# A top-1 expert stage on one Trainium2 core: every expert on all 576 tokens, or each on its 90 slots

## The chip, the cores and the metric

The kernel runs on one core of a Trainium2 chip (trn2). The metric is the device time of one execution in microseconds (us). Engine names are those of the profile: PE does matrix products, PEld loads PE's stationary operand, DVE is the vector engine, ACT the scalar engine, POOL the GpSimd engine, SP issues most DMAs. PSUM is the memory that PE writes, in 8 banks of 512 float32 columns; everything else lies in SBUF.

## The reference

The model is a small vision tower: 16 images of 36 patches give 576 tokens of 64 values, and four blocks of attention and feed-forward work follow, each with a layer norm behind it. The change is in the first feed-forward stage (`_L0_ffn_ref`), a top-1 mixture of 8 experts with a capacity:

```
C = max(1, math.ceil(CAPACITY_FACTOR * T / E))        # 1.25 * 576 / 8 = 90
idx = jnp.argmax(probs, axis=-1)
pos = (jnp.cumsum(one_hot, axis=0) * one_hot).sum(-1).astype(jnp.int32) - 1
kept = pos < C
buf = jnp.zeros((E, C, D), dtype=h.dtype).at[idx, pos_safe].set(x, mode='drop')
hmid = jax.nn.relu(jnp.einsum('ecd,edf->ecf', buf, w1) + b1[:, None, :])   # D 64, F 256
ybuf = jnp.einsum('ecf,efd->ecd', hmid, w2) + b2[:, None, :]
y_tok = ybuf[idx, pos_g] * (prb * kept)[:, None]
y = jnp.nan_to_num(y, nan=0.0, posinf=10000.0, neginf=-10000.0)
```

## The kernel before

The kernel is one program, `tower`, with the instructions of each engine written out by hand in the order in which the engine runs them. Semaphores (`S["..."]`) order the engines among themselves; nothing is scheduled for it. Activations lie transposed, 64 features by 288 tokens twice: the first 288 tokens on partitions 0 to 63 and the others on 64 to 127 (`rows(h)`). In token order there are 6 tiles of 96 tokens (`TT` is 96).

Each norm goes the same way: ACT squares the sum in PSUM (L905), PE sums the squares (L424), ACT takes a root (L910), DVE a reciprocal (L1118), PE spreads it over the partitions (L432, in `spread`), DVE multiplies (L1123). `idle(n, bank)` (L417) is n matmuls of 512 columns on zeros whose result nobody reads.

The first expert stage is `ffn(0, HP)`. The router gives logits (L450), DVE finds each token's expert (`top_first`) and its softmax gate, and PE counts with a triangular matrix how many tokens chose the same expert before (L493, L496); a token beyond 90 gets gate 0. The gates are split in three bf16 parts, turned by PE (L504) and copied by DVE (L1150). Then all 8 experts work on all 576 tokens, in 16 chunks of 128 hidden values: `up` (L464) multiplies, ACT applies relu (L925), `gate` (L471) spreads the expert's gate over 128 partitions in PSUM, DVE multiplies (L1203), `down` (L477) adds into one PSUM bank. DVE replaces values that aren't finite (L1315 to L1322, the guard), and PE adds the centred result to the residual (L655). The next norm begins there.

POOL computes tables for a recurrence that comes two stages later (`lru_*`: L357 to L377, 45 instructions, one after the other by semaphore; L357 works on 576 columns, most others on 1 to 36). Ahead of them in its order stand the rope tables (L350, L352) and `gates32(0)` (L325), which waits until DVE has copied the turned gates of this stage.

## Time and profile before

| | |
|---|---|
| median of 3 runs | 156.04 us (155.33 to 158.31) |
| span of the profiled execution | 153.6 us |
| PE busy | 139.1 us, 91% |
| DVE, ACT, POOL busy | 97.4, 71.6, 34.8 us |

The time of a run also holds what lies before and behind the span; against the median that is 2.4 us. Times in the trace count from the start of the span. A PE matmul on float32 is two records. An instruction's record holds a fixed part in which the next one has already begun, so rates are read from the starts of a series or from its whole length, not from the mean of one.

### The profile page before, as it was taken

To read this page: it belongs to the slowest core of one execution; us is meant where nothing else is said; L and a number is where in the kernel's file an instruction comes from. 1 tells how busy PE (TensorE), PEld (TensorE's weight loads), DVE (VectorE), ACT (ScalarE), POOL (GpSimd) and SP (SyncE) were. 2 spreads that over 40 slices of the span, in tenths; PEclk is the share of its full clock that TensorE was granted. 3 is DMA by queue.
4 is the path that set the end of the run, shared out by engine and by line. 5 is a ranking of instruction groups with operands and counts; after the bars stand their busy time and mean duration, and the time that the engine had idled before them with its cause. 6 is when DMAs were issued, how large, how long until landed. Compare 5 with 4: busy or idle time off the path is not lost.

```text
span 153.6 us, 2957 instructions
## 1 busy us (share of the span) xinstructions
PE 139.1 (91%) x1132; PEld 72.8 (47%) x1145; DVE 97.4 (63%) x299; ACT 71.6 (47%) x136; POOL 34.8 (23%) x91
## 2 busy tenths in 40 slices
PE   6999999899999999698999977999899999999970
PEld 1455465645454344164355333547354464654550
DVE  6405858755466736756677899755758468314992
ACT  3645951675647010059244202434881366458452
POOL 8704000037777100002600004300087000000000
PEclk9999999999999999999999999999999999999999
DMA  5999991000000000000002000000000000000001
GB/s 154 353 426 382 264 358 54 0 0 2 6 0 2 0 0 0 4 0 0 0 3 59 0 2 0 0 4 0 4 0 0 0 0 6 0 0 4 0 0 38
DMA packets 3716, 8.17 MB, mean 53 GB/s; under 512 B 1579, under 2 KB 1707, under 8 KB 3574
## 3 DMA queue, kind: packets, MB, share of 16 engines
q1 hardware_dynamic: 3390, 7.87, 15.0%
q8 instruction: 9, 0.15, 0.4%
q10 hardware_dynamic: 312, 0.11, 0.3%
q14 instruction: 5, 0.04, 0.1%
HBM read 7.61 MB, written 0.15 MB: 51 GB/s over the span
## 4 chain that ended last, share of the span: by engine, by line
PE 65%; DVE 22%; ACT 5%; issue 4%; DMA 2%; DVEq 0%; ACTq 0%
PE ps L477 10%; PE ps L464 9%; PE ps L417 9%; PE ps L471 4%; PE ps L424 3%; DVE scores L1383 3%; DVE residual L1504 3%; PE ps L432 2%; DMA weights_sb<-weights 2%; DVE patch_sb L1496 2%; PE ps L582 2%; PE ps L574 2%; PE ps L446 2%; DVE scores_rest L1404 2%; ACT hidden L925 1%
## 5 line engine op out<-in xcount | busy, mean ns | idle before, releaser
L417 PE MATMUL ps<-idle_operand 128*128 128x512 bf16 x111 | 31.7, 394 | 4.7 <-DVE scores L1383 1.6
L1203 DVE TENSOR_TENSOR hidden_gated<-hidden,ps 128x576 f32<-128x576 f32 x28 | 19.7, 750 | 10.5 <-PE ps L471 10.5
L925 ACT ACTIVATE hidden<-ps,weights_sb 128x576 f32<-128x576 f32 x28 | 19.6, 738 | 9.9 <-PE ps L464 8.2
L917 ACT ACT_TABLE_LOAD x16 | 20.5, 1283 | 0.3
L417 PEld LDWEIGHTS ps<-idle_operand 128*128 128x128 bf16 x124 | 10.4, 102 | 17.3 <-issue 3.7
L905 ACT ACTIVATE squares<-ps 128x288 f32<-128x288 f32 x7 | 2.9, 411 | 28.9 <-PE ps L672 8.4
L477 PE MATMUL ps<-hidden_gated,weights_sb 128*64 128x288 f32 x112 | 16.3, 418 | 0.0
L325 POOL CAST combine_parts_T<-combine_parts_T 64x288 f32<-64x288 bf16 x3 | 1.3, 418 | 55.3 <-DVE combine_parts_T L1150 55.3
L464 PE MATMUL ps<-h,weights_sb 64*128 64x288 f32 x80 | 13.0, 436 | 0.7 <-ACT hidden L925 0.4
L1115 DVE COPY centred<-ps 128x288 f32<-128x288 f32 x7 | 3.2, 457 | 11.9 <-ACT squares L905 11.9
L477 PEld LDWEIGHTS ps<-hidden_gated,weights_sb 128*64 128x64 f32 x112 | 6.7, 135 | 7.0 <-DVE hidden_gated L1203 2.7
L856 PE MATMUL ps<-weights_sb,hidden 128*128 128x256 f32 (+2 forms) x28 | 9.8, 473 | 0.0
L464 PEld LDWEIGHTS ps<-h,weights_sb 64*128 64x128 f32 x80 | 6.7, 185 | 5.9 <-ACT hidden L925 3.2
L1383 DVE TENSOR_REDUCE scores<-ps 128x32 f32<-128x512 f32 (+1 forms) x13 | 7.7, 652 | 0.7 <-PE ps L724 0.7
L471 PE MATMUL ps<-combine_parts_T,selectors 128*128 128x288 bf16 x40 | 7.4, 289 | 0.0
L424 PEld LDWEIGHTS ps<-consts_sb,squares 128*96 128x96 f32 x48 | 4.7, 164 | 3.9 <-ACT squares L905 3.4
L432 PE MATMUL ps<-consts_sb,rstd 96*64 96x96 f32 x108 | 6.2, 253 | 0.1
L464 PE MATMUL ps<-xn,weights_sb 64*128 64x288 f32 x32 | 5.5, 446 | 0.5 <-ACT hidden L925 0.4
L432 PEld LDWEIGHTS ps<-consts_sb,rstd 96*64 96x64 f32 x108 | 4.7, 136 | 2.4 <-DVE rstd L1118 2.1
L856 PEld LDWEIGHTS ps<-weights_sb,hidden 128*128 128x128 f32 (+1 forms) x28 | 4.6, 183 | 2.4 <-issue 1.6
L389 POOL TENSOR_TENSOR patch_sb<-scores,top 128x288 f32<-128x288 f32 (+1 forms) x2 | 1.6, 782 | 18.2 <-DVE top L1392 18.1
L471 PEld LDWEIGHTS ps<-combine_parts_T,selectors 128*128 128x128 bf16 x40 | 3.0, 97 | 5.3 <-issue 1.9
(309 smaller groups left out, 235.7 us busy)
## 6 DMA issues: line engine op xcount, KB each, us to landing
patch_sb<-patches SPq DMA_DIRECT2D x6, 288.0 KB, 5.5
weights_sb<-weights SPq DMA_DIRECT2D x1, 1108.0 KB, 10.1
weights_sb<-weights SPq DMA_DIRECT2D x1, 717.0 KB, 15.1
weights_sb<-weights SPq DMA_DIRECT2D x1, 689.0 KB, 13.8
weights_sb<-weights SPq DMA_DIRECT2D x1, 640.0 KB, 7.6
weights_sb<-weights SPq DMA_DIRECT2D x1, 512.0 KB, 13.5
...
```

The source lines that it names most:

```text
L417: mm(PS[:, bank, :], idle_in[:, 0:P], idle_in[:, :], start=True, stop=True)
L424: last = mm(psVar[:, 2 * t:2 * t + 2], SQ[:, cols(t)], c("mean"), start=True, stop=True)
L432: last = mm(dst[rows(h), cols(t)], RS[:, at + 2 * t + h:at + 2 * t + h + 1].to_broadcast([TT, D]), c("ident", TT)[:, 0:TT], start=True, st ...
L464: last = mm(PS[:, z + h, 0:HALF], w1[rows(h), ch, :], src[rows(h), :], start=True, stop=True)
L471: last = mm(PS[:, bank + h, 0:HALF], sel[:, g, h, :], CT3[:, :], start=True, stop=True)
L477: last = mm(PS[rows(h), YB, 0:HALF], w2[:, ch, :], HG[:, ch % GRING, h, :], start=False, stop=(ch == chunks - 1), skip_group_check=True)
L856: return mm(y3(q, a, b), tok3(q, ch), wd[:, ch, a * E:b * E], start=False, stop=(ch == 1), skip_group_check=True)
L917: act.activation(warm[:, tables[0]:tables[0] + 1], warm[:, 0:1], func)
L925: act.activation(HR[:, at % RING, :, :], two(ZA if ch % 2 == 0 else ZB), func, bias=w(f"b1_{n}")[:, ch:ch + 1]).then_inc(S["act_out"], 1)
L1203: dve.tensor_tensor(HG[:, at % GRING, :, :], HR[:, at % RING, :, :], two(GATE_AT[n][ch]), ALU.mult)\
L1383: dve.tensor_reduce(SC[:, j, :, 8 * g:8 * g + keys].rearrange("p h s -> p s h"), PS[:, n % 4, 0:keys * D].rearrange("p (s h d) -> p s h d" ...
L1504: ins = dve.tensor_reduce(R[0:p, q, a:b], YM[0:p, q, a:b, :], AX, ALU.add)
```

## The change

Each expert now works on its 90 slots alone. Experts 0 to 3 lie on partitions 0 to 63 and experts 4 to 7 on 64 to 127.

- Slot numbers: the counting matmuls get one more (L645 of the new kernel) that adds 1024 times the expert's number, so that the count read at a token's own expert is a number that names expert and slot. DVE takes it out (two instructions).
- Gather: for each of the 6 token tiles a one-hot matrix of 96 tokens by 720 slots is made by comparing a table `IO` with the slot numbers (5 on DVE, 1 on POOL); PE multiplies the normalised tokens by it (`dispatch`). The tokens in token order come from 3 new PE transposes and 6 ACT copies that also scale them.
- Experts: `up` and `down` on 90 columns per expert; the biases come in through matmuls of 4 rows and of 1 row (`before_up`, `before_down`). ACT takes one half of the relu, DVE the other.
- Return: PE spreads the slot numbers over the partitions (`slot_b`), ACT copies them, and 8 one-hot matrices of 90 slots by 576 tokens are made (`put_rows`, 5 on DVE, 3 on POOL); `bring_back` multiplies by them. DVE first bounds the experts' outputs to finite values (`finite`), and the gate is multiplied behind it.
- The splitting and turning of this stage's gates goes, and with it `gates32(0)`. Two DMAs of small bias rows and one of `IO` (270 KB) are added, and `w1_0` is loaded once instead of on both halves (512 KB less).

```diff
-    ("gate_w", 2 * E), ("gb0", E), ("b1_0", 2 * E), ("b2_0", P), ("w1_0", 2 * E * P),
+    ("gate_w", 2 * E), ("gb0", E), ("w1_0", E * P),
...
+DT = HR[0:CAP, :, :, :]
...
+DS = [x_flat[0:TT, i * SLOTS:(i + 1) * SLOTS] for i in range(IN_X)] \
...
+XK = sb("x0_tok", [TT, 2 * NT, D])
...
+SLB = KP[:, :].rearrange("p (h n) -> p h n", h=2)
+XD = sb("x0_slots", [P, SLOTS // 2])
+HD = [[x[:, 0:4 * CAP] for x in pair] for pair in ((U, B1), (B2, UC))]
...
+PUT_DVE, PUT_POOL = [0, 1, 4, 3, 6], [5, 2, 7]
+POOL_TILE = 2 * NT - 1
...
+def put_rows(engine, e):
+    return engine.tensor_scalar(DT[:, e, :, :].rearrange("p h n -> p (h n)"), token_ids(),
+                                c("slot_id", CAP)[:, e:e + 1], None, ALU.is_equal)
...
+    sp.dma_start(IO[:, :], iota).then_inc(S["iota0"], 16)
...
-    gates32(0)
...
+    pool.wait_ge(S["iota0"], 16)
+    pool.wait_ge(S["slot"], 1)
+    pool.tensor_scalar(DS[POOL_TILE], IO[:, :], slot[:, POOL_TILE:POOL_TILE + 1], None, ALU.is_equal)\
+        .then_inc(S["disp_pool"], 1)
+    pool.wait_ge(S["slot_in"], 1)
+    for e in PUT_POOL:
+        put_rows(pool, e).then_inc(S["put_pool"], 1)
     gates32(1)
...
-        bank = MB if k == 4 else ZA
+        bank = {1: YB, 4: MB}.get(k, ZA)
...
-            gate(0, G)
...
-            for pair in range(1, E - 2):
-                gate(pair, G, 2 * pair - 1)
-                down(2 * pair - 2)
-                down(2 * pair - 1)
...
-            gate(E - 2, ZA)
...
-            gate(E - 1, ZB)
-            for ch in range(chunks - 6, chunks):
-                down(ch)
...
+    def experts0():
...
+        def before_up(s):
+            for g in range(2):
+                mm(PS[:, 2 * s + g, 0:4 * CAP].rearrange("p (j n) -> p j n", j=4),
+                   BR0[0:4, (2 * s + g) * P:(2 * s + g + 1) * P],
+                   c("ident")[0:4, 0:4].unsqueeze(2).to_broadcast([4, 4, CAP]),
...
+        def dispatch(i):
+            if i == POOL_TILE:
+                pe.wait_ge(S["disp_pool"], 1)
+            else:
+                pe.wait_ge(S["disp_dve"], i + 1)
+            for g in range(2):
+                last = mm(psD[rows(g), :], XK[:, i, :], DS[i][:, g * slots:(g + 1) * slots],
...
+        def up(s):
+            pe.wait_ge(S["xd_in"], s + 1)
+            for r in range(2):
+                for ch in range(2):
+                    for g in range(2):
+                        j = 2 * r + ch
+                        last = mm(PS[:, 2 * s + g, j * CAP:(j + 1) * CAP], w1[rows(g), 2 * s + r, ch, :],
+                                  XD[rows(g), (2 * s + r) * CAP:(2 * s + r + 1) * CAP],
...
+            last.then_inc(S["z0"], 1)
+        def before_down(s):
+            mm(psS[s].rearrange("p (g f) -> p g f", g=2), ones[32:33, 0:CAP], staged(BR0[32:33, :])[:, s],
...
+        def down(s):
+            for g in range(2):
+                pe.wait_ge(S["h0_act" if g == 0 else "h0_dve"], s + 1)
+                for r in range(2):
+                    e = 4 * g + 2 * s + r
+                    for ch in range(2):
+                        last = mm(psS[s][:, (2 * g + r) * D:(2 * g + r + 1) * D], HD[s][g][:, (2 * r + ch) * CAP:(2 * r + ch + 1) * CAP], w2[:, e, ch, :],
...
+            last.then_inc(S["ys_done"], 1)
+        def bring_back(s):
+            pe.wait_ge(S["ys_in"], s + 1)
+            for g in range(2):
+                for r in range(2):
+                    e = 4 * g + 2 * s + r
+                    sem, count = putter(e)
+                    pe.wait_ge(S[sem], count)
+                    for h in range(2):
+                        last = mm(psBack[rows(h), :], YS[:, e, :], DT[:, e, h, :],
...
+        idle(4, YB)
...
+        pe.wait_ge(S["onehot"], 1)
...
+        mm(psN, tri[0:1, 0, :], cb("slot_base", 1).rearrange("p (i e) -> p i e", e=E),
...
+        mm(psN, tri[:, 1, :], ohb[:, :, :], start=False, stop=False, skip_group_check=True)
+        for k in range(2 * NT - 1):
+            later = 2 * NT - 1 - k
+            last = mm(psN[:, k + 1:2 * NT, :], tri[:, 0, :],
+                      ohb[:, k, :].unsqueeze(1).to_broadcast([TT, later, E]),
...
+        last.then_inc(S["counted"], 1)
+        pe.wait_ge(S["rows0"], 32)
+        pe.wait_ge(S["x0_ready"], 2 * NT)
+        before_up(0)
+        pe.wait_ge(S["slot"], 1)
+        for h in range(2):
+            for t in range(NT):
+                i = h * NT + t
+                last = mm(PS[:, ZB + h, cols(t)], slot[:, i:i + 1].to_broadcast([TT, P]), c("ident", TT)[:, 0:TT],
...
+        last.then_inc(S["slot_b"], 1)
+        for i in range(3):
+            dispatch(i)
+        before_down(0)
+        dispatch(3)
+        dispatch(4)
+        pe.wait_ge(S["slot_in"], 1)
+        before_up(1)
+        dispatch(5).then_inc(S["xd_done"], 1)
+        up(0)
+        up(1)
+        pe.wait_ge(S["gate0"], 1)
+        for t in range(NT):
+            for h in range(2):
+                last = mm(psBC[rows(h), cols(t)], m6[3][0:TT, 2 * t + h:2 * t + h + 1].to_broadcast([TT, D]),
...
+        last.then_inc(S["gate0_b"], 1)
+        pe.wait_ge(S["w_f0b"], 16)
+        down(0)
+        pe.wait_ge(S["gate0_in"], 1)
+        before_down(1)
+        down(1)
+        bring_back(0)
+        bring_back(1).then_inc(S["back"], 1)
...
+        last = pe.transpose(PS[0:TT, ZA, t * P:(t + 1) * P], XC[:, cols(t)], c("ident"))
+    last.then_inc(S["x0_t"], 1)
     spread(1)
-    pe.wait_ge(S["w_f0b"], 16)
-    pe.wait_ge(S["hp"], 2)
-    ffn(0, HP)
+    experts0()
+    residual("ident")
     idle(2, ZA)
...
+    act.wait_ge(S["x0_t"], 1)
+    act.wait_ge(S["rs"], 2)
+    for t in range(NT):
+        for h in range(2):
+            act.activation(XK[:, h * NT + t, :], PS[0:TT, ZA, t * P + h * D:t * P + (h + 1) * D], ACT.Copy,
+                           scale=RS[:, 2 * t + h:2 * t + h + 1]).then_inc(S["x0_ready"], 1)
     table(ACT.Exp)
     act.wait_ge(S["exp_in"], 1)
     act.activation(ex[0:TT, :, :], t8[0][0:TT, :, :], ACT.Exp).then_inc(S["exp_out"], 1)
-    act.wait_ge(S["w_f0"], 16)
-    hidden(0, ACT.Relu, range(2 * E))
+    act.wait_ge(S["slot_b"], 1)
+    act.activation(SLB[:, :, :], two(ZB), ACT.Copy).then_inc(S["slot_in"], 1)
     table(ACT.Sqrt)
+    act.wait_ge(S["xd_done"], 1)
+    for s in range(2):
+        act.activation(XD[:, 2 * s * CAP:2 * (s + 1) * CAP], psD[:, 2 * s * CAP:2 * (s + 1) * CAP], ACT.Copy)\
+           .then_inc(S["xd_in"], 1)
+    for s in range(2):
+        act.wait_ge(S["z0"], s + 1)
+        act.activation(HD[s][0], PS[:, 2 * s, 0:4 * CAP], ACT.Relu)\
+           .then_inc(S["h0_act"], 1)
+    act.wait_ge(S["gate0_b"], 1)
+    act.activation(PB[:, :], psBC, ACT.Copy).then_inc(S["gate0_in"], 1)
...
+    def experts0():
...
+        dve.wait_ge(S["counted"], 1)
+        link(dve.tensor_tensor(count, psN, ohb[:, :, :], ALU.mult))
+        dve.tensor_reduce(slot[:, :], count, AX, ALU.add).then_inc(S["slot"], 1)
+        dve.wait_ge(S["slot"], 1)
+        dve.wait_ge(S["iota0"], 16)
+        for i in range(POOL_TILE):
+            dve.tensor_scalar(DS[i], IO[:, :], slot[:, i:i + 1], None, ALU.is_equal).then_inc(S["disp_dve"], 1)
+        dve.wait_ge(S["exp_out"], 1)
+        link(dve.tensor_reduce(m6[2][0:TT, :], ex[0:TT, :, :], AX, ALU.add))
+        dve.reciprocal(m6[3][0:TT, :], m6[2][0:TT, :]).then_inc(S["gate0"], 1)
+        dve.wait_ge(S["slot_in"], 1)
+        def put(n):
+            put_rows(dve, PUT_DVE[n]).then_inc(S["put_dve"], 1)
+        def relu(s):
+            dve.wait_ge(S["z0"], s + 1)
+            dve.tensor_scalar(HD[s][1], PS[:, 2 * s + 1, 0:4 * CAP], 0.0, None,
+                              ALU.max).then_inc(S["h0_dve"], 1)
+        def finite(s):
+            dve.wait_ge(S["ys_done"], s + 1)
+            step(dve.tensor_scalar(YP[:, s, :], psS[s], 0.0, SAT, ALU.max, ALU.min))
...
+            sync()
+            dve.tensor_tensor(staged(YS[:, :, :].rearrange("p e d -> p (e d)"))[:, s], YP[:, s, :].rearrange("p (g f) -> p g f", g=2),
...
+                              ALU.add).then_inc(S["ys_in"], 1)
+        put(0)
+        put(1)
+        put(2)
+        relu(0)
+        put(3)
+        relu(1)
+        put(4)
+        finite(0)
+        finite(1)
+        dve.wait_ge(S["gate0_in"], 1)
+        dve.wait_ge(S["back"], 1)
+        step(dve.tensor_tensor(RY[:, :], psBack, PB[:, :], ALU.mult))
+        step(dve.tensor_scalar(nf[:, :], psBack, LIMIT_A, LIMIT_B, ALU.mult, ALU.mult))
+        sync()
+        link(dve.tensor_scalar(RX[:, :], nf[:, :], 1.0e4, None, ALU.mult))
+        dve.copy_predicated(RY[:, :], nf[:, :], RX[:, :]).then_inc(S["guarded"], 1)
...
     link(dve.tensor_reduce(m6[0][0:TT, :], lg[0:TT, :, :], AX, ALU.max))
+    top_first(None, lg, m6[0], t8[1], m6[1], TT, 2 * NT)
+    dve.tensor_tensor(in_order(ohb[:, :, :]), by_tile(t8[1][0:TT, :, :]), by_tile(col(m6[1], TT, 2 * NT)), ALU.is_equal)\
+       .then_inc(S["onehot"], 1)
     dve.tensor_tensor(t8[0][0:TT, :, :], lg[0:TT, :, :], col(m6[0], TT, 2 * NT), ALU.subtract)\
        .then_inc(S["exp_in"], 1)
     normalise(1, HP[:, :], "hp")
-    top_first(t8[2], lg, m6[0], t8[1], m6[1], TT, 2 * NT)
-    dve.tensor_copy(in_order(ohb[:, :, :]), by_tile(t8[2][0:TT, :, :])).then_inc(S["onehot"], 1)
-    dve.wait_ge(S["exp_out"], 1)
-    link(dve.tensor_reduce(m6[2][0:TT, :], ex[0:TT, :, :], AX, ALU.add))
-    link(dve.reciprocal(m6[3][0:TT, :], m6[2][0:TT, :]))
-    link(dve.tensor_tensor(comb[0:TT, :, :], t8[2][0:TT, :, :], col(m6[3], TT, 2 * NT), ALU.mult))
-    dve.wait_ge(S["counted"], 1)
...
-    link(dve.tensor_tensor(comb[0:TT, :, :], comb[0:TT, :, :], t8[1][0:TT, :, :], ALU.mult))
...
-    gate_hidden(0)
-    dve.wait_ge(S["y_done"], 2 * E)
-    dve.tensor_copy(RY[:, :], psY).then_inc(S["guard_read"], 1)
-    dve.wait_ge(S["guard_read"], 1)
-    step(dve.tensor_scalar(np_[:, :], RY[:, :], FMAX, 1.0e4, ALU.is_gt, ALU.mult))
-    step(dve.tensor_scalar(nm[:, :], RY[:, :], -FMAX, 1.0e4, ALU.is_lt, ALU.mult))
-    step(dve.tensor_scalar(nf[:, :], RY[:, :], 0.0, 0.0, ALU.mult, ALU.not_equal))
-    sync()
-    link(dve.tensor_tensor(np_[:, :], np_[:, :], nm[:, :], ALU.subtract))
-    dve.copy_predicated(RY[:, :], nf[:, :], np_[:, :]).then_inc(S["guarded"], 1)
...
```

On PE, in the middle of the stage, this stood in a row before (`up`, `gate`, `down` in turn):

```order
L464 MATMUL ps<-h,weights_sb 128x288 x4
L471 MATMUL ps<-combine_parts_T,selectors 128x288 x2
L477 MATMUL ps<-hidden_gated,weights_sb 64x288 x4
L464 MATMUL ps<-h,weights_sb 128x288 x4
L471 MATMUL ps<-combine_parts_T,selectors 128x288 x2
L477 MATMUL ps<-hidden_gated,weights_sb 64x288 x4
```

and this stands there now, from the counting to the first matmuls of `up`:

```order
L589 MATMUL ps<-consts_sb,bias_rows 128x360 x2
L661 MATMUL ps<-consts_sb,slot_of_token 128x96 x6
L600 MATMUL ps<-patch_sb,x_tok 64x360 x6
L616 MATMUL ps<-bias_rows,ones 90x256
L600 MATMUL ps<-patch_sb,x_tok 64x360 x2
L600 MATMUL ps<-hidden_gated,x_tok 64x360 x2
L589 MATMUL ps<-consts_sb,bias_rows 128x360 x2
L600 MATMUL ps<-hidden_gated,x_tok 64x360 x2
L610 MATMUL ps<-x_slots,weights_sb 128x90 x16
```

The last `dispatch` (on the tile that POOL makes) stands right ahead of `up`.

On POOL, behind the rope tables, this stood before:

```order
L350 TENSOR_SCALAR rope_tables<-consts_sb,weights_sb 128x36 x4
L352 TENSOR_TENSOR rope_tables<-rope_tables 128x36
L325 CAST combine_parts_T<-combine_parts_T 64x288
L357 TENSOR_SCALAR decay<-decay,lru_par 128x576
L358 COPY lru_sin_sb<-lru_par 128x1
```

and now:

```order
L391 TENSOR_SCALAR rope_tables<-consts_sb,weights_sb 128x36 x4
L393 TENSOR_TENSOR rope_tables<-rope_tables 128x36
L396 TENSOR_SCALAR decay<-decay,lru_par 128x576
L397 COPY lru_sin_sb<-lru_par 128x1
L398 TENSOR_SCALAR lru_t<-lru_par 128x1
```

Nothing now stands between the rope tables and the recurrence tables. Behind those, on POOL, the new work stands in a row:

```order
L415 TENSOR_SCALAR rot_out_c<-lru_cos,consts_sb 128x36
L416 TENSOR_SCALAR rot_out_s<-lru_sin_sb 128x36
L420 TENSOR_SCALAR hidden_gated<-slot_iota,slot_of_token 96x720
L303 TENSOR_SCALAR hidden<-kp,consts_sb 90x576 x3
L366 CAST combine_parts_T<-combine_parts_T 64x288
```

So POOL's part of the gather and of the return comes only when all recurrence tables are done.

## Rows read from the trace of the kernel before

**Rows 1.** The page: busy time by engine, and the granted clock in 40 slices.
```profile
PE 139.1 (91%) x1132; PEld 72.8 (47%) x1145; DVE 97.4 (63%) x299; ACT 71.6 (47%) x136; POOL 34.8 (23%) x91
...
PEclk9999999999999999999999999999999999999999
```
**Rows 2.** Groups by form, 26 to 56 us: count | busy us, mean ns | idle before.
```profile
L1203 DVE TENSOR_TENSOR hidden_gated<-hidden,ps 128x576 f32<-128x576 f32 x16 | 11.3, 750 | 7.3 <-PE ps L471 7.2
...
L464 PE MATMUL ps<-h,weights_sb 64*128 64x288 f32 x64 | 10.3, 435 | 0.3 <-DVE h L1123 0.2
L477 PE MATMUL ps<-hidden_gated,weights_sb 128*64 128x288 f32 x64 | 9.4, 419 | 0.0
```
**Rows 3.** Timeline of PE, 24 to 60 us: start, length, what.
```profile
27.73 0.71 PE L432 MATMUL ps<-consts_sb,rstd 96*64 96x96 f32 x12
...
30.38 0.22 PE L493 MATMUL ps<-onehot_bf,bconsts_sb 96*96 96x48 bf16 x1
...
42.91 1.24 PE L464 MATMUL ps<-h,weights_sb 64*128 64x288 f32 x8
44.08 0.42 PE L471 MATMUL ps<-combine_parts_T,selectors 128*128 128x288 bf16 x2
44.43 1.19 PE L477 MATMUL ps<-hidden_gated,weights_sb 128*64 128x288 f32 x8
45.55 1.24 PE L464 MATMUL ps<-h,weights_sb 64*128 64x288 f32 x8
...
54.61 0.75 PE L655 MATMUL ps<-guard_y,consts_sb 128*128 128x288 f32 x2 [0.17 <-DVE guard_y L1322]
```
**Rows 4.** Timeline of DVE, 24 to 60 us.
```profile
29.92 0.18 DVE L1303 CAST onehot_bf<-gate_tmp 96x48 bf16<-96x48 f32 x1
...
30.92 0.20 DVE L1309 TENSOR_SCALAR gate_tmp<-ps 96x48 f32<-96x48 f32 x1 [0.24 <-PE ps L496]
...
52.31 0.46 DVE L1315 COPY guard_y<-ps 128x288 f32<-128x288 f32 x1 [0.81 <-PE ps L477]
52.80 0.31 DVE L1317 TENSOR_SCALAR plus_inf<-guard_y 128x288 f32<-128x288 f32 x1
...
54.07 0.48 DVE L1322 COPY_PREDICATED guard_y<-nonfinite,plus_inf 128x288 f32<-128x288 int32 x1
```
**Rows 5.** Timelines of PE elsewhere, for rates: one series each.
```profile
7.54 3.12 PE L582 MATMUL ps<-patch_sb,weights_sb 128*64 128x288 f32 x23
...
22.36 1.98 PE L629 MATMUL ps<-kernel_T,v_sb 36*128 36x36 f32 x32 [0.36 <-DVE kernel_T L1258]
...
98.39 1.31 PE L757 MATMUL ps<-consts_sb,probs 128*128 128x128 f32 x10
...
126.77 2.11 PE L417 MATMUL ps<-idle_operand 128*128 128x512 bf16 x9 [0.16 <-issue]
```
**Rows 6.** Timeline of ACT: 4 copies that scale by a column.
```profile
149.06 1.12 ACT L1071 ACTIVATE out_sb<-residual,gate_col 64x64 f32<-64x64 f32 x4
```
**Rows 7.** Timeline of POOL: rope tables, and first and last of the recurrence.
```profile
12.92 0.26 POOL L352 TENSOR_TENSOR rope_tables<-rope_tables 128x36 f32<-128x36 f32 x1
...
33.46 1.72 POOL L357 TENSOR_SCALAR decay<-decay,lru_par 128x576 f32<-128x576 f32 x1
...
50.31 0.30 POOL L377 TENSOR_SCALAR rot_out_s<-lru_sin_sb 128x36 f32<-128x36 f32 x1
```
**Rows 8.** Timelines of DVE and PE, 13 to 18 us.
```profile
13.70 0.43 DVE L1225 TENSOR_SCALAR xn<-q_rot,weights_sb 128x288 f32<-128x288 f32 x1
14.28 1.24 PE L593 MATMUL ps<-xn,weights_sb 64*128 64x288 f32 x8
...
16.00 0.76 DVE L1246 TENSOR_TENSOR kp<-base_sb,rope_tables 128x576 f32<-128x576 f32 x1 [0.86 <-ACT base_sb L945]
17.46 0.76 DVE L1249 TENSOR_TENSOR k_rot<-kp,ks 128x576 f32<-128x576 f32 x1
```
**Rows 9.** Timelines of DVE and POOL, 94 to 98 us.
```profile
94.66 0.32 DVE L1396 TENSOR_TENSOR patch_sb<-top 128x160 f32<-128x160 f32 x1
94.70 0.87 POOL L389 TENSOR_TENSOR patch_sb<-scores,top 128x320 f32<-128x320 f32 x1
...
96.81 0.72 POOL L396 TENSOR_TENSOR patch_sb<-patch_sb,row_stat 128x320 f32<-128x320 f32 x1
```

More of the change, by code:

```diff
@@ L84 @@
 zero3 rows_c wo_c cen_c wr_gam wr_bet_mm wr_bet rows_zero still topped replaced filled idrep
+iota0 rows0 x0_t x0_ready slot slot_b slot_in disp_dve disp_pool xd_done xd_in z0 h0_dve h0_act ys_done ys_in
+put_dve put_pool gate0 gate0_b gate0_in back
 acc sq xc var sd rs bc hp xn
@@ L1195, in gate_hidden @@
             def gate_hidden(n):
-                chunks, gate_of = FFN[n]
-                for ch in range(chunks):
+                for ch in range(FFN[n]):
                     at = BASE[n] + ch
@@ L1666, in _pack, with _rows0 @@
     return pk
+def _rows0(b1, b2):
+    by_bank = b1.reshape(2, 2, 2, 2, P).transpose(2, 3, 1, 0, 4)
+    return np.concatenate([by_bank.reshape(4, 4 * P), b2.reshape(1, E * D)], 0).astype(np.float32)
 def kernel(**inputs):
@@ L1683 @@
         "maskk": mask,
+        "iota": np.tile((SLOT_STEP * np.arange(E)[:, None] + np.arange(CAP)[None, :] + 1).reshape(1, -1), (TT, 1))
+        .astype(np.float32),
+        "rows0": _rows0(i["L0_ffn_b1"], i["L0_ffn_b2"]),
         "bias3": np.tile(i["L3_ffn_bd"].T.reshape(1, -1), (3, 1)).astype(np.float32),
```

139 lines of the change are left out of this document (75 added, 64 removed).

## The prediction

> **What bounds the kernel now.** I read the page first. PE is busy for 91% of the span, DVE for 63%, and the granted clock is at its full level (2.4 GHz) in every slice [rows 1]. A busy share doesn't say what ends last, so the chain of waits came next: in this stage it runs through `up`, `gate` and `down` (L464, L471, L477) almost without a break. The groups by form say why: `up` and `down` are 64 records each, with 0.3 us and nothing of idle time ahead of them, while DVE sits idle for 7.3 us before L1203 [rows 2]. So the stage is PE's. The timeline gives its frame: the first count starts at 30.38, the matmul that ends the stage (L655) at 54.61, and between them one turn of the loop takes 45.55 - 42.91 = 2.64 us [rows 3]. Behind the last `down` come 2.3 us of guard, from 52.31 to 54.61 [rows 3, 4]. The result's place is the start of the centre matmul; what lies behind it is the same work in both kernels, on the same chain, and I move it as a block.
>
> **Rates.** L582 runs pairs of 288 float32 columns on half-width tiles: 12 matmuls (one record of 24 is missing) in 3.12 us, less a tail of 0.2 (L493 lasts 0.22 for almost no columns), give 0.49 a pair, 1.7 ns a column [rows 3, 5]. Where columns are few, loading the stationary operand sets the pace: L757 has 128 columns on either side and takes (1.31 - 0.2) / 10 = 0.11 a record; L629 moves only 36 columns under 128-wide weights on alternating halves of the rows, and takes (1.98 - 0.2) / 32 = 0.056 [rows 5]. An idle matmul is (2.11 - 0.2) / 9 = 0.21 [rows 5]. The loop's turn holds 4 pairs (1.96) and two bf16 matmuls (0.24); the 0.44 left over fall on three changes of tile shape, 0.15 each [rows 3].
>
> A rule speaks against the change here: the Trainium skill, page TensorEngine Tiling (Array Packing), section Tiling Modes, says that changing the tiling mode drains the engine. The trace agrees in kind (0.15 us over at each change); the page gives no figure. With no cost for a change the sum below would be 1.8 us shorter.
>
> **Part 1, up to the slot numbers.** Three transposes stand ahead of the spreading of the reciprocals, 3 x 0.11: it starts at 27.73 + 0.33 = 28.06 instead of 27.73 [rows 3] and lasts 0.5. Now 6 idle matmuls follow where 2 did: 1.27, so PE is ready to count at 29.85. The one-hot was ready at 30.10 [rows 4]; now a copy is folded into the comparison, and the subtraction for the exponential and the multiplication of L1123 stand behind it, about 0.2 + 0.2 + 0.4, so that it is there at about 29.3. The idle matmuls, not DVE, now hold up the count. From the first count to DVE's reading it were 30.92 - 30.38 = 0.54 [rows 3, 4]; with one more, 0.6. Two small DVE instructions make the slots: about 30.95. PE has 1.2 us of `before_up(0)` to do meanwhile. That one also needs ACT's six copies: four of that kind took 1.12, so 0.28 each [rows 6], from 28.6 at the latest to 30.3, when PE comes to them: just hidden. Were they later, each tenth would count.
>
> **Part 2, PE from there.** Each bias matmul of 360 columns is 0.61, although it has only 4 rows; each `dispatch` is a pair of 360 columns, 0.61.
> - `before_up(0)`: 0.15 + 1.22, from 30.25 to 31.6.
> - slot numbers, 12 records of 128-wide weights: 0.15 + 1.3, to 33.1.
> - six `dispatch` 3.67, `before_down(0)` 0.43, `before_up(1)` 1.22, five changes of shape 0.75: to 39.2.
> - hop to ACT and back (tail 0.2, a copy of 180 columns some 0.3, start 0.05): to 39.75. Nothing covers it.
> - `up`, 32 records at 0.056: to 41.5. Gates 0.15 + 0.5: to 42.15. The relus (some 0.5 on each engine) lie under these.
> - `down`, 32 records of 90-wide weights, 0.11 x 90 / 128 = 0.08: 2.5, with 0.43 of bias and three changes: to 45.55.
> - `bring_back`, 8 pairs of 288 columns: 0.15 + 3.92, to 49.6, and the tail to 49.8.
> - Guard: the copy out of PSUM goes; two readings of PSUM (0.46, the second about 0.39 behind the first), one 0.31, one 0.48, with the hops 1.7 [rows 4]: the centre matmul starts at 51.55.
>
> That is 54.61 - 51.55 = 3.05 us earlier. By the rates, the stage before was 32 pairs, 16 bf16 matmuls and one bias matmul, 18.1 us of columns; now it is 2.4 + 1.3 + 3.7 + 0.9 + 1.8 + 0.5 + 2.5 + 3.9 = 17.0. Gathering, returning and the biases eat what 720 rows of expert work instead of 4608 save.
>
> **Part 3, DVE and POOL in the stage.** Five comparisons of 720 columns: L1225, with two column operands on 288 columns, took 0.43 [rows 8], and L1317, with none, 0.31 [rows 4]. The bound for one is so 0.5 (double rate) to 0.9 (single), and even at 0.9 the five are ready at 31.9, 32.8, 33.7, 34.6 and 35.5, before PE wants each (33.3, 33.9, 34.5, 35.7, 36.3), each by at least 0.8. The matrices for the return and `finite` also fall before PE needs them: `finite(0)` starts at 43.8 and takes 1.3, PE wants it at 45.55. Where DVE falls back by a microsecond this shows at once.
> POOL makes one dispatch tile: 1.72 x 720 / 576 = 2.15 us [rows 7]. Its recurrence tables took 50.61 - 33.46 = 17.15 us [rows 7]. They don't wait for `gates32(0)` any more, so they start at 13.2, end at 30.35 undisturbed, and the tile is there at 33.1, where PE wants it at 38.6: 5.5 us of cover.
> The DMAs: 0.5 MB less, 0.27 more, and all queue behind what the beginning needs. Nothing.
>
> **Part 4, what the earlier start of POOL collides with.** At 13.2 the 1.72 us instruction of POOL (L357) now runs while DVE does L1225 at 13.70, for which PE's L593 at 14.28 waits directly [rows 8]. Before, DVE's work beside L357 was the multiplication out of PSUM. Can the two disturb each other? One place shows it: DVE's L1396, with two operands in SBUF, starts at 94.66, POOL's L389 at 94.70 and it takes 0.87, where the same size takes 0.72 at 96.81 [rows 9]. POOL gave way by 0.15. That DVE gives way when POOL is first no row shows. So the bounds for L1225: 0, and waiting for POOL's end (14.9 instead of 13.70), 1.2, of which PE feels 1.1. I take the upper one, since the one collision on record looks like waiting, not like sharing. `kp`, `ks` and `k_rot` (16.00 to 18.2) would meet short POOL instructions: 0.3 together. Sum 1.4 us lost at 14 to 18 us, against 3.05 won.
>
> The Trainium skill, page SBUF — State Buffer, section SBUF: two separate sides, states that GpSimd and DVE share a port pair under an exclusive lock, held for the whole instruction, against DVE instructions in a two-port mode or with two SBUF inputs; the loser blocks fully. The 0.15 us agree with it, and no row here shows its other direction. By this rule the upper bound holds; without it the lower.
>
> **Forecast.** 3.05 - 1.4 = 1.65 us off the span of 153.6; off the median of 156.04 (which holds 2.4 us around the span, untouched) that is 154.4 us.
>
> **Rivals.**
> - No collision: DVE's L1225 isn't held. Then 156.04 - 3.05 = 153.0. For it: no row of a delayed DVE instruction. Against it: rows 9.
> - Changes of shape are cheap when the next operands are ready: 0.05 instead of 0.15 at 12 of them, 1.2 less: 153.2 with the collision, 151.8 without. For it: `gate` waits on semaphores in the loop, which may be part of the 0.44.
> - POOL is late, slower than before. Every DVE instruction with two SBUF operands or at double rate between 13 and 36 us (some 9.5 us of them, 5 x 0.76 in 16 to 20 alone) holds POOL's chain for its length. Tables to 39.9, tile to 42.0, where PE wants it at 38.6 + 1.4 = 40.0: 2.0 more, 156.4. It decides from a tile at 41.7 on. Against it: POOL lost only 0.15 to a DVE instruction of 0.32, and gaps lie between DVE's.
> - Loads not hidden in `up` and `down`: columns come on top, 1.2 and 1.7 us: 157.3 with the collision, 155.9 without. Against it: L629's 0.056, which is under load plus columns.
> - That the change doesn't shorten the expert work can't be: `up` goes from 64 to 32 records and from 288 to 90 columns.
>
> **Chances.** Forecast 0.38, no collision 0.26, cheap changes 0.18, POOL late 0.10, loads exposed 0.08. A measurement of this kernel tells about 2%, 3.1 us, from no change: below 152.9 lie half of the second, two thirds of the third and a little of the first, 0.32 together; above 159.2 lies little, 0.03. The range from 151.5 to 156.9 leaves out about a tenth on either side.
>
> **What would show it.** The first matmul on `xn` (L593 before) starting at 15.4 instead of 14.28, with a DVE instruction of about 1.6 us before it; no wait of PE between the count and the hop at 39 (plus the shift); the last `dispatch` not waiting on POOL; centre matmul at 53.0. Wrong I would be if DVE's comparisons come later than PE's pairs, or if the 4-row matmuls run at another pace than their columns.

## The result: 8% slower

The changed kernel takes 168.25 us in the median of four runs (167.69 to 168.47), the kernel before 155.69 beside it (155.02 to 158.31): a ratio of 1.083, interval 1.079 to 1.088. Some executions of one kernel, that of 158.31 us among them, run slower at a lower mean clock (down to 0.96 in the kernel before), and the ratios in this document leave them out. The prediction was 154.4 us, with 151.5 to 156.9 as its range.

The page of the changed kernel, the lines that answer to [rows 1]: busy time by engine, and the granted clock in 40 slices of 4.2 us.

```profile
PE 151.6 (91%) x1143; PEld 82.5 (50%) x1156; DVE 92.5 (55%) x292; ACT 64.3 (39%) x132; POOL 47.7 (29%) x94
...
PEclk9999999955555555899999999999999999999999
```

PE is busy for 91% of the span, as before. The clock isn't full any more: eight slices stand at half. The windows tell where (stretch, PE busy and records, granted clock, DMA share, GB/s):

```profile
32.00:33.60 1.60, 1.60 (x15) 1.00 0.02 5
33.60:34.00 0.40, 0.40 (x4) 0.81 0.00 0
34.00:66.00 32.00, 31.36 (x143) 0.50 0.00 1
66.00:68.00 2.00, 2.00 (x5) 0.51 0.00 0
68.00:70.00 2.00, 2.00 (x23) 1.00 0.00 0
```

From 33.9 us to about 68 the clock is at 1.2 GHz, and PE is at work in all of it but 0.6 us. From 30 us to the fall it is busy without a break, so no pause of PE stands behind it. The timeline of PE, which answers to [rows 3]:

```profile
30.61 1.48 PE L589 MATMUL ps<-consts_sb,bias_rows 4*128 4x360 f32 x4
...
40.73 2.76 PE L589 MATMUL ps<-consts_sb,bias_rows 4*128 4x360 f32 x4
...
45.31 3.72 PE L610 MATMUL ps<-x_slots,weights_sb 64*128 64x90 f32 x32 [0.42 <-ACT x_slots L1093]
...
56.49 7.95 PE L637 MATMUL ps<-hidden,q_rot 90*64 90x288 f32 x32
...
66.35 1.27 PE L773 MATMUL ps<-guard_y,consts_sb 128*128 128x288 f32 x2
```

Two bias matmuls of the same shape (L589, 4 records) take 1.48 us at 30.61 and 2.76 at 40.73. The centre matmul (L773) starts at 66.35, where it stood at 54.61 [rows 3]: 11.7 us of the span's 13.0 (153.6 to 166.6). The rest lies behind: the last half-clock matmuls up to 68, and 0.7 us that PE waits ahead of the first scores for the DMA of the keys.

What the prediction had feared at the start doesn't show. DVE (L1351) and POOL (L396) there, for [rows 8]:

```profile
13.74 0.43 DVE L1351 TENSOR_SCALAR xn<-q_rot,weights_sb 128x288 f32<-128x288 f32 x1
```
```profile
12.84 1.85 POOL L396 TENSOR_SCALAR decay<-decay,lru_par 128x576 f32<-128x576 f32 x1
```

DVE's `xn` takes 0.43 as before, in the middle of POOL's instruction.

### The profile page after: what moved, and what is told of

Read it like the earlier page. It is cut to its first block, busy times and chain, and to the rows that moved or that the text cites. A ratio compares the mean times of both kernels' runs of the same rounds, so it can differ in the third digit from the quotient of the medians.

```text
span 166.6 us, 2947 instructions
## 1 busy us (share of the span) xinstructions
PE 151.6 (91%) x1143; PEld 82.5 (50%) x1156; DVE 92.5 (55%) x292; ACT 64.3 (39%) x132; POOL 47.7 (29%) x94
## 4 chain that ended last, share of the span: by engine, by line
PE 71%; DVE 19%; ACT 3%; issue 3%; DMA 2%; ACTq 0%; DVEq 0%
PE ps L464 11%; PE ps L637 5%; PE ps L600 5%; PE ps L524 4%; PE ps L511 3%; PE ps L625 3%; PE ps L479 3%; PE ps L471 3%; DVE scores L1542 3%; PE ps L589 2%; DVE residual L1663 2%; DMA k_parts_img<-k_parts_tok 2%; PE ps L610 2%; PE ps L518 2%; PE ps L693 2%
## 5 line engine op out<-in xcount | busy, mean ns | idle before, releaser
L366 POOL CAST combine_parts_T<-combine_parts_T 64x288 f32<-64x288 bf16 x2 | 0.8, 418 | 54.9 <-DVE combine_parts_T L1277 54.9
L1329 DVE TENSOR_TENSOR hidden_gated<-hidden,ps 128x576 f32<-128x576 f32 x12 | 8.4, 751 | 3.3 <-PE ps L518 3.3
L1043 ACT ACTIVATE hidden<-ps,weights_sb 128x576 f32<-128x576 f32 x12 | 8.5, 737 | 2.4 <-PE ps L511 2.1
L637 PE MATMUL ps<-hidden,q_rot 90*64 90x288 f32 x32 | 7.9, 691 | 0.0
L1443 DVE TENSOR_SCALAR base_sb<-ps 128x360 f32<-128x360 f32 x1 | 0.5, 532 | 11.7 <-PE ps L610 11.7
L524 PE MATMUL ps<-hidden_gated,weights_sb 128*64 128x288 f32 x48 | 6.9, 417 | 0.0
L493 PE MATMUL ps<-h,consts_sb 128*128 128x288 f32 x14 | 5.7, 495 | 0.0
L471 PE MATMUL ps<-consts_sb,squares 128*96 128x2 f32 x48 | 5.3, 227 | 0.1
L838 PE MATMUL ps<-bconsts_sb,q_parts 128*128 128x512 bf16 (+1 forms) x13 | 4.8, 369 | 0.7 <-DMA k_parts_img<-k_parts_tok 0.7
```

What stands on the lines that cost most here:

```text
L471: last = mm(psVar[:, 2 * t:2 * t + 2], SQ[:, cols(t)], c("mean"), start=True, stop=True)
L524: last = mm(PS[rows(h), YB, 0:HALF], w2[:, ch, :], HG[:, ch % GRING, h, :], start=False, stop=(ch == chunks - 1), skip_group_check=True)
L637: last = mm(psBack[rows(h), :], YS[:, e, :], DT[:, e, h, :], start=(s == g == r == 0), stop=(s == g == r == 1), skip_group_check=True)
L1043: act.activation(HR[:, at % RING, :, :], two(ZA if ch % 2 == 0 else ZB), func, bias=w(f"b1_{n}")[:, ch:ch + 1]).then_inc(S["act_out"], 1)
L1329: dve.tensor_tensor(HG[:, at % GRING, :, :], HR[:, at % RING, :, :], two(GATE_AT[n][ch]), ALU.mult)\
```

## The experiments

**Theory A.** The new stage's matmuls use few rows of the array (4 and 1 in the biases, 96 and 90 in the gather and the return), and with such work PE doesn't keep its clock, busy or not. **Theory B.** Something else halves it: a new operation as such, or the other engines. A second question was the 1.4 us that the prediction charged to POOL and DVE.

### First set: idle work, no biases, more rows

**e1_idle.** Behind each piece of the stage, as here:

```diff
                 before_up(0)
+                idle(2, YB)
```

> The changed kernel with eleven idle matmuls (128 x 128 on 512 columns of bfloat16, about 0.22 us each at full clock) put into the first expert stage, on a bank that is free there: two each behind the bias rows before up, behind the slot broadcast, behind the first three dispatches and behind the second bias, one each behind up, behind the first half of down and between the halves of bring_back. They add at most 2.4 us of TensorE's time. Theory A (the granted clock falls because the new matmuls use few rows or columns of the array, and full ones hold it): the clock stays 1.00 in every slice, the stage keeps its full-clock lengths, and the kernel takes 154 to 158 us. Theory B (the clock falls for a reason that other matmuls in the stage don't touch, such as the total of the work or the other engines): it falls again near 34 us and the kernel takes 169 to 171 us.

167.87 and 170.54 us in its two runs, before 155.54 beside it. A miss for A as I had put it:

```profile
34.00:34.50 0.50, 0.50 (x5) 0.57 0.00 0
37.00:38.00 1.00, 1.00 (x8) 0.76 0.00 0
38.00:44.00 6.00, 5.44 (x25) 1.00 0.00 0
44.00:45.00 1.00, 0.98 (x12) 0.66 0.00 0
46.00:66.00 20.00, 19.52 (x98) 0.50 0.00 0
```

The clock falls at 34.1 all the same, but comes back at 37.5, stays full for 6.8 us and falls again at 44.3. So the added matmuls do something, and not enough; B's "falls again" is met too. e13 comes back to this.

**e2_nobias.**

```diff
-                before_up(0)
...
-                before_down(0)
...
-                                          start=False, stop=True, skip_group_check=True)
+                                          start=True, stop=True, skip_group_check=True)
```

> The changed kernel without the matmuls of the two biases of the first expert stage (four of 4 rows and two of 1 row are left out, and with them both biases, so the output is another); up and down start their sums themselves. Theory A1 (the matmuls of 4 rows and of 1 row alone bring the clock down): it stays 1.00 and the kernel takes 150 to 153 us. Theory A2 (the slot broadcast and the dispatches, 96 rows by 64 columns of the array, bring it down too): it still falls, near 34 us, and the kernel takes 162 to 167 us.

160.46 us. The clock falls at 33.4, a little earlier than with the biases, is full from 36.9 to 40.3, and falls again. So A1, "the few-row matmuls alone", doesn't hold as stated. But taking the biases away also opened a pause: PE is busy for only 1.38 us of the two from 30 to 32, where it had been busy throughout. The run can't tell a pause from few rows. It shows that the clock can fall in this stage without any bias matmul.

**e3_rows** and **e4_biasrows.** The decisive pair, here the biases of up (`before_up`); the added rows hold zeros:

```diff
-                           BR0[0:4, (2 * s + g) * P:(2 * s + g + 1) * P],
-                           c("ident")[0:4, 0:4].unsqueeze(2).to_broadcast([4, 4, CAP]),
+                           BR0[:, (2 * s + g) * P:(2 * s + g + 1) * P],
+                           c("ident")[:, 0:4].unsqueeze(2).to_broadcast([P, 4, CAP]),
```

> The changed kernel with all 128 rows in the bias matmuls, the slot broadcast, the dispatches and bring_back: the added rows of the operands hold zeros (or meet zeros), so the result is that of the changed kernel, the columns and the number of instructions are the same, and only the rows of the array that are used grow (4, 1, 96 and 90 to 128). Theory A, in the form that used rows count: the clock stays 1.00 throughout and the kernel takes 152 to 156 us. In the form that what counts is the data (rows of zeros do nothing), or the columns of the array (dispatch and bring_back write 64 of 128): the clock falls as before and it takes 167 to 170 us. Setting more rows to zero on VectorE at the start costs under 1 us.

> The changed kernel with 128 rows (all but 4 or 1 of them zero) in the bias matmuls alone; the slot broadcast, the dispatches and bring_back keep 96 and 90 rows. Theory A1 (the 4-row and 1-row matmuls are the cause, by their used rows): the clock stays 1.00 and it takes 152 to 156 us. Theory A2 (the dispatches matter as well): the clock falls, if later than 33.9 us, and it takes 162 to 169 us.

e4_biasrows took 153.88 us, 14.4 less than the change, with the same instructions in the stage. Its clock, and its stage:

```profile
32.00:34.00 2.00, 2.00 (x18) 1.00 0.01 4
34.00:50.00 16.00, 15.58 (x141) 1.00 0.01 1
50.00:58.00 8.00, 7.03 (x45) 1.00 0.01 2
```
```profile
30.45 0.22 PE L647 MATMUL ps<-bconsts_sb 1*96 1x48 bf16 x1
...
30.89 1.46 PE L591 MATMUL ps<-consts_sb,bias_rows 128*128 128x360 f32 x4
...
33.60 2.04 PE L602 MATMUL ps<-patch_sb,x_tok 96*64 96x360 f32 x12
...
37.52 1.48 PE L591 MATMUL ps<-consts_sb,bias_rows 128*128 128x360 f32 x4
...
40.18 2.02 PE L612 MATMUL ps<-x_slots,weights_sb 64*128 64x90 f32 x32 [0.42 <-ACT x_slots L1095]
...
45.91 4.10 PE L639 MATMUL ps<-hidden,q_rot 90*64 90x288 f32 x32
...
51.87 0.75 PE L775 MATMUL ps<-guard_y,consts_sb 128*128 128x288 f32 x2 [0.74 <-DVE guard_y L1474]
```

The clock is 1.00 throughout. The first bias takes 1.46 us with 128 rows where it took 1.48 with 4; the second one 1.48 instead of 2.76, `up` (L612) 2.02 instead of 3.72, `bring_back` (L639) 4.10 instead of 7.95. The centre matmul starts at 51.87. It is one run, but the 22 runs of e9_late, e10_lessidle, e12_hop and e14_dvetile below, which build on it, have mean clocks of 0.97 to 1.00, and the four of the changed kernel 0.89 to 0.90. That is Theory A in the form of used rows, with one limit: the 96 and 90 rows of gather and return do no harm once the biases are full. The data can't be it, since what was added is zeros. e3_rows took 157.65 (156.91 and 158.38; ratio 1.013, 1.002 to 1.025): the clock is full in the whole stage, which lasts 21.41 us from count to centre, as in e4_biasrows (21.42). But my zeroing of memory ahead of the first centring on VectorE kept the start back. PE stood idle for 3 us there, and the patch matmuls, 3.1 us at full clock [rows 5], took 5.6 at 0.50. This loss at 10 us isn't the stage's, and my "under 1 us" for it was wrong.

### Second set: which of them, and without the change

**e5_bu0** and **e6_disprows** split e3's edit the other way: the one gives 128 rows to the first bias alone, the other to slots, dispatch and return alone.

```diff
+                    n = P if s == 0 else 4
                     for g in range(2):
...
-                           BR0[0:4, (2 * s + g) * P:(2 * s + g + 1) * P],
+                           BR0[0:n, (2 * s + g) * P:(2 * s + g + 1) * P],
```

```diff
-                        last = mm(psD[rows(g), :], XK[:, i, :], DS[i][:, g * slots:(g + 1) * slots],
+                        last = mm(psD[rows(g), :], XK[:, i, :], DF[i][:, g * slots:(g + 1) * slots],
```

(`DF` is `DS` on 128 partitions, and `XK` has 32 rows of zeros more.)

> The changed kernel with 128 rows (all but 4 of them zero) in the first bias of up alone, the two matmul pairs that stand just ahead of the slot broadcast; the second bias of up keeps 4 rows and the two biases of down 1 row. Memory is set to zero on VectorE where it idles, so the start isn't delayed. If the place ahead of the fall at 33.9 us is all that matters, the clock stays 1.00 to the end and it takes 153 to 154 us. If every stretch in which few-row matmuls stand together with 96-row ones brings the clock down, it stays up past 33.9 us and falls later, at the 1-row bias and the second 4-row bias (37 to 42 us) or in bring_back, and it takes 158 to 166 us.

> The changed kernel with 128 rows in the slot broadcast, the dispatches and bring_back (the added rows are zeros), and the biases left at 4 rows and 1 row: the mirror of the run in which the biases alone have 128. If the biases' few rows are enough to bring the clock down, it falls near 34 us as in the changed kernel, and it takes 160 to 169 us. If the sum of used rows over the stretch decides, so that 32 and 38 more rows in the long pieces make up for the biases, the clock stays 1.00 and it takes 152 to 156 us.

The kernel before took 158.31 us in its single run beside these four, at the upper end of its spread (154.6 to 158.8 in all sets), so they are read by clock and trace. e5_bu0 took 162.11, and its clock falls at 40.4 instead of 33.9; e6_disprows took 160.08, and it falls at 41.0:

```profile
40.00:40.40 0.40, 0.40 (x8) 1.00 0.00 0
40.40:40.80 0.40, 0.40 (x10) 0.56 0.00 0
41.20:44.00 2.80, 2.80 (x30) 0.50 0.03 6
```
```profile
40.00:41.00 1.00, 0.65 (x12) 1.00 0.00 0
41.00:41.50 0.50, 0.50 (x10) 0.53 0.00 0
42.00:44.00 2.00, 2.00 (x22) 0.50 0.00 0
```

More rows in the first bias alone, or in the dispatches alone, carry the clock past 34 us. Neither carries it past the second 4-row bias (37 to 39 us), the 1-row bias and the 0.42 us of waiting that follow. e5 does what its second case says; e6 does what neither of its two says. So no single instruction is the culprit: the few-row pieces of a stretch and the 96-row ones add up. Whether the 0.42 us pause has a part in it, no run isolates.

**e7_before4** and **e8_before128**, with nothing of the change in them:

```diff
+            for _ in range(8):
+                mm(PS[:, ZA, 0:360], c("ident")[0:4, :], w("w1_0")[0:4, 0:360], start=True, stop=True)
             ffn(0, HP)
```

> The kernel before with eight added matmuls on 360 columns of float32 just ahead of its first expert stage, whose result nobody reads, with 4 rows of the array used: nothing of the change is in it. At full clock they take 2.5 to 3.0 us together, so about 158 us if the clock holds. The theory (few-row matmuls bring the clock down by themselves) expects a fall to 0.50 within or behind them, for at least some microseconds, and 159 to 170 us. If the clock needs the rest of the new stage to fall, it stays 1.00.

> The control to the run with eight added matmuls of 4 rows: the same eight in the same place of the kernel before, with 128 rows used. Every theory expects the clock at 1.00 in every slice and 157.5 to 158.5 us, the 155.6 of before and 2.5 to 3.0 for the eight.

166.92 and 160.24 us, one run each. The added series, with 4 rows and with 128:

```profile
29.63 8.50 PE L650 MATMUL ps<-weights_sb,consts_sb 4*128 4x360 f32 x16 [0.22 <-DVE h L1125]
```
```profile
28.98 5.08 PE L650 MATMUL ps<-weights_sb,consts_sb 128*128 128x360 f32 x16 [0.22 <-DVE h L1125]
```
The clock, in e7_before4 around its fall and in e8_before128 over the whole stretch:

```profile
30.50:31.00 0.50, 0.50 (x3) 1.00 0.00 0
31.00:31.50 0.50, 0.50 (x3) 0.60 0.00 0
31.50:32.00 0.50, 0.50 (x3) 0.50 0.00 0
```
```profile
29.00:45.00 16.00, 15.87 (x89) 1.00 0.01 2
```

The same sixteen records take 8.50 us with 4 rows and 5.08 with 128. With 4 the clock falls at 31.1, 1.5 us into the series, and is full again from 44.8 on, in the old stage; PE is busy all that time. With 128 rows it is full from 29 to 45. Both are longer than I expected since I had taken 0.31 us for a matmul that takes 0.63 (two records); the 5.08 also explains the control's time (155.6 and 5.1 are 160.7). Four rows are enough, with nothing of the new stage around them. It is a single run, in which the clock might have fallen for another reason; that the fall comes inside the added series speaks for the rows, and the comparison of e4_biasrows with the changed kernel doesn't rest on it.

### Third set: what is left once the clock holds

**e9_late**: the zeroing behind the centring, the rows' DMAs behind the stage's second load. **e10_lessidle**: also `idle(4, YB)` ahead of the count becomes `idle(1, YB)`. **e12_hop**: also the gates' broadcast moves ahead of up(0).

```diff
-            sp.dma_start(BR0[0:4, :], rows0[0:4, :]).then_inc(S["rows0"], 16)
...
             load("f0b", "w_f0b")
+            sp.wait_ge(S["zero0"], 2)
+            sp.dma_start(BR0[0:4, :], rows0[0:4, :]).then_inc(S["rows0"], 16)
```

```diff
-                idle(4, YB)
+                idle(1, YB)
                 pe.wait_ge(S["bconst"], 16)
```

```diff
                 dispatch(5).then_inc(S["xd_done"], 1)
-                up(0)
-                up(1)
                 pe.wait_ge(S["gate0"], 1)
                 for t in range(NT):
...
                 last.then_inc(S["gate0_b"], 1)
+                up(0)
+                up(1)
```

> The kernel with 128 rows in the biases of the first stage alone (as in the run that took 153.88 us), with two changes of place: the memory for them is set to zero on VectorE behind the early centring instead of ahead of it, and their rows are loaded behind the second part of the stage's weights. The first kept the start back by 0.35 us. The clock stays 1.00, and it takes 153.3 to 153.9 us, 0.98 to 0.99 of before.

> The same with one idle matmul instead of four ahead of the count. The one-hot was ready at 29.8 us and the count began at 30.45, behind the idle ones. If the 128-row biases leave room, the clock stays 1.00, all that follows moves by 0.6 us, and it takes 152.7 to 153.4 us. If the idle matmuls were needed to hold the clock through the slot broadcast and the dispatches, it falls between 32 and 41 us and it takes over 158 us.

> The kernel with one idle matmul ahead of the count, with the gates' broadcast (0.72 us of TensorE) put ahead of the first up instead of behind both. It then stands in the 0.42 us in which TensorE waits for the dispatched tokens to be copied. Everything behind moves by 0.3 to 0.4 us: 152.4 to 153.1 us, 0.980 to 0.985 of before, if the clock stays up.

Against 155.50 of before in the same set (12 runs): e9_late 152.73, ratio 0.983 (0.979 to 0.987); e10_lessidle 152.52, 0.981 (0.977 to 0.985); e12_hop 151.86, 0.978 (0.975 to 0.981). All three are below the times expected, e10 by 0.2 us, e9 and e12 by over 0.5 us. The profile of e9 lacks a wait of 1.1 us for a DMA behind the stage, which that of e4_biasrows has (more on it under "Behind the stage"). In e12 `up` starts 1.25 us behind the sixth dispatch (38.51 and 39.76), as in e10 (38.86 and 40.10): the whole broadcast fits into the hop and saves 0.65 us, not 0.3 to 0.4. e10's expected 0.6 us didn't come, and the timelines of PE and POOL say why:

```profile
29.40 0.19 PE L647 MATMUL ps<-bconsts_sb 1*96 1x48 bf16 x1
...
36.44 1.48 PE L591 MATMUL ps<-consts_sb,bias_rows 128*128 128x360 f32 x4
38.86 0.83 PE L602 MATMUL ps<-hidden_gated,x_tok 96*64 96x360 f32 x4 [0.94 <-POOL hidden_gated L422]
```
```profile
36.71 2.10 POOL L422 TENSOR_SCALAR hidden_gated<-slot_iota,slot_of_token 96x720 f32<-96x720 f32 x1
```

The count starts 0.46 us earlier than in e9_late (29.86), but the sixth dispatch waits 0.94 us for POOL's tile, ready at 38.81. That is the rival "POOL is late", covered by only 0.36 us in e4_biasrows (tile at 38.57, dispatch at 38.93). In e9_late it struck already: the tile is ready at 38.47, and the sixth dispatch starts at 38.53, 1.60 us behind the bias ahead of it, where e4_biasrows has 1.41.

**e14_dvetile** makes that tile on VectorE and takes it from POOL:

```diff
-            pool.tensor_scalar(DS[POOL_TILE], IO[:, :], slot[:, POOL_TILE:POOL_TILE + 1], None, ALU.is_equal)\
-                .then_inc(S["disp_pool"], 1)
...
+                dve.tensor_scalar(DS[POOL_TILE], IO[:, :], slot[:, POOL_TILE:POOL_TILE + 1], None, ALU.is_equal)\
+                   .then_inc(S["disp_pool"], 1)
                 dve.wait_ge(S["slot_in"], 1)
```

> The kernel of the run with the gates' broadcast in the hop (one idle matmul ahead of the count, 128-row biases), with the sixth comparison tile made on VectorE behind its reciprocal, at about 34.5 us for 0.5 us, instead of on GpSimd at 36.1 to 38.2 us. TensorE can no longer wait for GpSimd there. In the profiled execution of the hop run that tile came 0.3 us before it was needed, in the one before 0.94 us late. Where it was late the time falls by up to 0.9 us: 151.0 to 152.0 us in the median, 0.970 to 0.978 of before. If the wait was no part of most executions, the ratio stays at 0.978.

152.19 us, ratio 0.977 (0.972 to 0.981). The tile takes 0.55 us at 33.95 on DVE and the wait can't occur. Against e12_hop (0.978) nothing can be told; there the tile was in time in the profiled execution (38.15, wanted at 38.51), and e14's own profile has 0.99 us of waiting for the keys' DMA, which that of e12 hasn't. The best of these versions are 2.2 and 2.3% faster than before by their ratios, with intervals from 1.9 to 2.8%.

**e11_held**: the disputed collision by itself.

```diff
+            pool.wait_ge(S["k_ready"], 1)
             pool.wait_ge(S["lru_sin"], 2)
```

> The kernel of the run with late zeros, with GpSimd's rotation chain held back until VectorE has k_rot (about 18 us instead of 13). It tests the term of the prediction by which the chain's early start keeps VectorE back by 1.4 us. If that term is real, xn comes 1.1 us earlier than without the hold and the whole kernel 1.0 to 1.4 us. If only GpSimd gives way when both want the memory, VectorE's row ahead of the stage doesn't move, the time is the same within 0.3 us, and the chain, which no longer meets those multiplications, ends at 36 to 38 us, hardly later than without the hold.

160.56 us, ratio 1.033 (1.029 to 1.038). Slower, by neither theory's price. PE waits:

```profile
36.38 1.48 PE L592 MATMUL ps<-consts_sb,bias_rows 128*128 128x360 f32 x4
41.45 1.44 PE L603 MATMUL ps<-hidden_gated,x_tok 96*64 96x360 f32 x4 [3.58 <-POOL hidden_gated L423]
```
```profile
40.00:41.00 1.00, 0.00 (x0) 1.00 0.00 0
41.00:42.00 1.00, 0.55 (x2) 0.76 0.00 0
42.00:52.00 10.00, 9.59 (x71) 0.51 0.01 2
```

POOL's chain began 4.4 us later than in e9_late and ended at 39.3, over a microsecond later than the 38 expected at the latest, and its tile at 41.4. PE stood for 3.58 us, and behind that pause the clock fell for some 10 us. So POOL's early start, whose collision the prediction counted as a cost, is needed for the tile. On the collision itself, `xn` against POOL's long instruction (L398 there), first e9_late, then e12_hop:

```profile
13.37 0.66 DVE L1355 TENSOR_SCALAR xn<-q_rot,weights_sb 128x288 f32<-128x288 f32 x1
```
```profile
13.89 0.84 DVE L1355 TENSOR_SCALAR xn<-q_rot,weights_sb 128x288 f32<-128x288 f32 x1
```
```profile
12.85 1.72 POOL L398 TENSOR_SCALAR decay<-decay,lru_par 128x576 f32<-128x576 f32 x1
```

`xn` took 0.43 in e11_held, where POOL was still, and in the changed kernel, where it wasn't; 0.66 in e9_late and 0.84 in e12_hop. So a collision costs DVE 0 to 0.4 us. `kp`, `ks` and `k_rot` take 0.75 or 0.76 in all of them.

**e13_fill** asks whether e1's filling was of the wrong kind or too little: `idle(7, YB)` behind each bias of up, `idle(3, YB)` behind the first bias and first half of down.

```diff
                 before_up(0)
+                idle(7, YB)
```

> The changed kernel, biases at 4 rows and 1 row as in the change, with 21 idle matmuls (128 x 128 on 512 columns of bfloat16) in place of eleven: seven behind each bias of up, three behind the first bias of down and three behind the first half of down. They take some 4.5 us at full clock. If the amount of full-row work beside the few-row pieces decides, the clock stays 1.00 and the kernel takes 156.5 to 159 us. If idle matmuls of this kind don't count, it falls near 34 us as before and the kernel takes 170 to 174 us.

The expectation miscounts: they are 20. 157.71 us, and the clock holds:

```profile
30.95 1.48 PE L589 MATMUL ps<-consts_sb,bias_rows 4*128 4x360 f32 x4
32.37 1.68 PE L464 MATMUL ps<-idle_operand 128*128 128x512 bf16 x7
...
39.97 1.48 PE L589 MATMUL ps<-consts_sb,bias_rows 4*128 4x360 f32 x4
```
```profile
30.00:42.00 12.00, 12.00 (x65) 1.00 0.00 1
42.00:58.00 16.00, 14.84 (x130) 1.00 0.00 1
```

Idle matmuls on zeros do count, if there are enough of them. These also stand in other places than e1's, and it is one run, so the amount isn't told from the place. The time is about the 153.9 of e4_biasrows and the filling's 4 us. Rows of zeros inside the bias matmuls do the same for nothing.

## Why the prediction was wrong, point by point

**The step that failed** is the one where all the rest was made in rates at full clock: "the granted clock is at its full level (2.4 GHz) in every slice [rows 1]", and then "Each bias matmul of 360 columns is 0.61, although it has only 4 rows". The first sentence is a state of the kernel before, taken as a constant. The second is nearly true (1.48 us for two and a change, with 4 rows, 1.46 with 128), and stopped short: the rows hardly set the matmul's own time, but what follows runs at half clock. That cost 14.5 us of stage (66.35 against 51.87) with an unchanged list of instructions. None of the rivals had it; the only place where I looked at rows was their pace.

**The sum itself held.** In e4_biasrows the stage takes 21.42 us from count to centre; predicted were 29.85 to 51.55, 21.7. The pieces: first bias 1.31 (predicted 1.37), slot numbers 1.40 (1.45), `bring_back` 4.03 up to the residual (4.07), and 0.42 of waiting for ACT, of a hop put at 0.55. The gain was 54.61 - 51.87 = 2.74 of the predicted 3.05.

**No collision** was the better case: 0 to 0.4 us on `xn` instead of 1.1, none on `kp` to `k_rot` instead of 0.3. What the collision does is lengthen POOL: L407 at 16.12 in the changed kernel takes 1.42 us instead of some 0.3 and ends at 17.54, just behind DVE's `kp` and `ks` (16.04 to 17.47), and the whole chain ended at 36.2 and not at 30.35. The Trainium skill, page SBUF — State Buffer, section SBUF: two separate sides, has the loser block for the whole instruction. If `xn` is one of the instructions it names, as the prediction took it, that fits e12_hop, where `xn` ends at 14.73 and POOL's instruction at 14.57, and e14_dvetile (14.68 and 14.52), but not the changed kernel, where it ran 13.74 to 14.17 inside 12.84 to 14.69, nor e9_late (13.37 to 14.03 inside 13.13 to 14.86). What tells the cases apart no run shows.

**POOL late** was weighed at 0.10 with a cover of 5.5 us. The true cover was 0.36 us at full clock, since POOL gave way far more often than the one place with 0.15 had made me believe; it was a near miss, and in e9_late (0.19 us) and e10_lessidle (0.94) it struck.

**Changes of shape**: with 96 or 128 rows in slots, dispatch and return the stage is the same within 0.01 us, so going between 90 or 96 rows and 128 costs nothing. Four rows cost a little: from the first bias to the end of the slot numbers the changed kernel takes 2.91 us, still at full clock (30.61 to 33.52), and e4_biasrows 2.71 (30.89 to 33.60). The other changes aren't priced one by one; the sum with 0.15 a change came out 0.3 too long, and with none it would have been 1.5 too short. That rival isn't borne out. **Loads** stayed hidden: `up` took 1.95 from its start to the gates' broadcast, 1.8 by the sum, where the rival adds 1.2. `down` with its bias took 3.13, 3.4 by the sum, so the good total hides two small errors that cancel in part.

**Behind the stage** I moved everything "as a block". It gives back some of the gain: in e4_biasrows 30.9 us from centre to scores instead of 30.1, since PE waited 1.1 us for the keys' DMA. Its transfers on ACT's queue took 1.34 us in the median there and 0.83 before; in e9, e10 and e12 it was 0.81 or 0.82, and the 0.8 us were gone; e14_dvetile has such a wait again, 0.99 us. No run settles what makes them slow in some executions.

The Trainium skill, page TensorE: Matmul & The Clock Gate, section Part 1: The HAM clock gate, speaks of the clock as held by how busy the PE is, and warns of pauses. e3's start and e11 agree (half clock behind pauses of 3 and 3.6 us). The changed kernel doesn't: PE was busy for all but 0.6 of 34 us and stayed at half. The measurement decides: busy records aren't enough.
